# Sixteen tiles in chunks of 2, 3, 4, 4 and 3 instead of 4, 4, 4 and 4, and gathers in tens that wait one group behind

## The reference

```python
target = item_id_feat + gelu(_ln(item_emb_d128 @ mm_w + mm_b, mm_ln_g, mm_ln_b))
seq_emb = item_table[item_seq]                      # rows x 50 x 128
x = concatenate([t, seq_emb, t - seq_emb, t * seq_emb], axis=-1)
scores = relu(x @ aw1 + ab1) @ aw2 + ab2            # 512 -> 64 -> 1
weights = softmax(where(item_seq == 0, -1e9, scores), axis=1)
hist_feat = einsum('bs,bsd->bd', weights, seq_emb)
sparse = stack([like, view, item_id, item_img, hist])   # 5 fields
se = sparse * sigmoid(relu(mean(sparse) @ se_w1 + se_b1) @ se_w2 + se_b2)
bil = pairwise (se[i] @ bil_W[i]) * se[j]           # 10 fields
dnn_in = xc = concatenate([se, bil])                # 15 x 128 = 1920 columns
for i in range(2):
    xc = dnn_in * (xc @ cross_K[i] + cross_bias[i]) + xc
h = gelu(_ln(xc @ w1 + b1, ...)); h = gelu(_ln(h @ w2 + b2, ...))
return sigmoid(h @ w3 + b3)
```

## Time and profile before

| | us |
|---|---|
| median of 3 runs | 2170.15 |
| lowest and highest | 2168.94, 2171.7 |
| span of the profiled execution | 2187.8 |

### The profile page before, as it was taken

One profiled execution on the slowest core, in us unless ns is written; L12 is line 12 of the kernel. 1 busy time (PEld: TensorE's weight loads), 2 busy tenths in 40 slices (PEclk: granted clock), 3 DMA queues, 4 the chain that ended last, 5 costly groups with the idle time before them and its releaser, 6 DMA issues. The chain is left out here.

```text
span 2187.8 us, 32802 instructions
## 1 busy us (share of the span) xinstructions
PE 1951.8 (89%) x9608; PEld 1531.8 (70%) x9608; DVE 1332.7 (61%) x2213; ACT 903.1 (41%) x1963; POOL 901.3 (41%) x854
## 2 busy tenths in 40 slices
PE   1654553999999999999999999999999999999997
PEld 1433432777777787777777787777777888888885
DVE  3444444577677766666777665666777755445553
ACT  1332332344454434664444334654445343322223
POOL 6666666566566540555565610545552000000000
PEclk6755565999999999999999999999999999999998
DMA  4111111344343463333344452334433352333330
GB/s 155 43 45 46 42 45 39 110 113 121 105 122 103 133 207 89 85 97 107 109 122 121 119 189 80 89 95 123 121 107 92 106 172 84 87 99 98 97 89 20
DMA packets 99535, 220.31 MB, mean 101 GB/s; under 512 B 21648, under 2 KB 27040, under 8 KB 99232
## 3 DMA queue, kind: packets, MB, share of 16 engines
q1 hardware_dynamic: 62928, 136.90, 21.0%
q0 software_dynamic: 27136, 55.63, 9.9%
q10 hardware_dynamic: 9296, 25.70, 3.1%
HBM read 205.29 MB, written 12.85 MB: 100 GB/s over the span
## 5 line engine op out<-in xcount | busy, mean ns | idle before, releaser
L394 POOL DMA_INDIRECT e<-in_item_table,idx_all x800 | 853.0, 1066 | 703.6 <-issue 340.1
L1087 DVE TENSOR_TENSOR Wl<-raw,Wh 128x640 fp32r<-128x640 f32 (+1 forms) x420 | 338.1, 805 | 297.5 <-DVEq L1086 269.0
L771 ACT ACTIVATE Wh<-raw 128x640 fp32r<-128x640 f32 (+1 forms) x420 | 301.4, 722 | 506.7 <-ACTq L770 430.0
L519 PE MATMUL xps<-X0h,Wh 128*128 128x512 f32 x900 | 365.0, 406 | 6.7 <-issue 6.7
L519 PE MATMUL xps<-X1h,Wh 128*128 128x512 f32 x900 | 361.7, 402 | 1.6 <-PEq L513 1.6
L520 PE MATMUL xps<-X1l,Wh 128*128 128x512 f32 x900 | 352.6, 392 | 0.0
L521 PE MATMUL xps<-X1h,Wl 128*128 128x512 f32 x900 | 352.5, 392 | 0.0
L521 PE MATMUL xps<-X0h,Wl 128*128 128x512 f32 x900 | 352.4, 392 | 0.0
L520 PE MATMUL xps<-X0l,Wh 128*128 128x512 f32 x900 | 351.9, 391 | 0.0
L734 ACT ACTIVATE e<-e,pw 128x128 f32<-128x128 f32 x800 | 242.7, 388 | 15.5 <-ACTq L128 10.5
L519 PEld LDWEIGHTS xps<-X0h,Wh 128*128 128x128 f32 x900 | 170.0, 189 | 40.8 <-issue 8.7
(11 more groups left out here) (144 smaller groups left out, 2233.7 us busy)
## 6 DMA issues: line engine op xcount, KB each, us to landing
raw<-in_cross_K SPq DMA_DIRECT2D x360, 320.0 KB
raw<-in_w SPq DMA_DIRECT2D x60, 256.0 KB
e<-in_item_table,idx_all POOLq DMA_INDIRECT x800
dnn_scratch<-dn ACTq DMA_DIRECT2D x12, 960.0 KB
x1f<-dnn_scratch ACTq DMA_DIRECT2D x3, 2048.0 KB
x1f<-dnn_scratch ACTq DMA_DIRECT2D x3, 1792.0 KB, 14.8
dn<-in_embT SPq DMA_DIRECT2D x1, 1024.0 KB
img_scratch<-dn ACTq DMA_DIRECT2D x1, 1024.0 KB, 4.8
```

The costliest lines, as they stand in the source:

```text
L394: nc.gpsimd.indirect_dma_start(out=dst, out_offset=None, in_=table, in_offset=bass.IndirectOffsetOnAxis(ap=idx_all[:, t, s:s + 1], axis=0) ...
L519: m0 = mm(out, wh, Xh[:, 0:T, k, :], start=(k == 0), stop=False)
L771: af(Wh[:, split_slot(w), 0:n], raw[:, rs, 0:n], ACT.Copy).then_inc(hi_done, 1)
L1087: v.tensor_tensor(Wl[:, rs, 0:n], raw[:, rs, 0:n], Wh[:, slot, 0:n].bitcast(F32), ALU.subtract).then_inc(lo_done, 1)
```

## The change

The 16 tiles are split as 2, 3, 4, 4 and 3, five chunks instead of four; all buffers stay sized for four tiles, since `TPC` is the largest chunk. The gathers of the first five tiles (chunks 0 and 1) wait, after each group of ten is issued, for the group ahead of it in the tile; before, those of the first four tiles waited after each ten for these same ten. The gathers of the other tiles wait after each five for what has been issued in the group, as before.

```diff
@@ -16,7 +16,7 @@
-TILES = (4, 4, 4, 4)
+TILES = (2, 3, 4, 4, 3)
 CHUNKS = len(TILES)
@@ -412,9 +412,12 @@
                     for s in range(g * GRP, (g + 1) * GRP):
                         gather(e[:, s, :], table_d, t, s, e_landed[g])
-                        if (s + 1) % (GRP if t < TILES[0] else SUB) == 0:
+                        if t >= TILES[0] + TILES[1] and (s + 1) % SUB == 0:
 
                             pool.wait_ge(e_landed[g], (t * GRP + s + 1 - g * GRP) * DMA)
+                    if t < TILES[0] + TILES[1] and g:
+
+                        pool.wait_ge(e_landed[g - 1], (t + 1) * (DMA * GRP))
```

## The result

The changed kernel takes 2220.47 us (median of 4 runs, 2216.51 to 2225.77), the kernel before on the same chip 2170.93 (2168.94 to 2171.76). The ratio is 1.0229, with a 95% interval of 1.0212 to 1.0247: slower by 2.3%. The forecast was 2167, its range 2124 to 2208. The profiled execution of the changed kernel took 2217.7 us, 2.1 more than its span.

What follows compares the result with a forecast made beforehand. TensorE bound the old chunks and GpSimd the opening; VectorE would bind the first new chunk, GpSimd the second. Terms 197 + 328 + 425 + 478 + 452 + 305 = 2185 us of span, less 17.6, gave 2167; range 2124 to 2208.

Steps and rivals of the forecast that it cites:

- Opening: Attention alone before the first chunk, now two tiles with fewer gather stalls: the first chunk starts at 197 us.
- Rival D: Opening: gathers in tens don't speed up, as each gather may grow without the stalls; opening 214, time 2184 us; chance 0.10.
- Product cadence: TensorE's spacing of products in the narrower chunks: 0.121 us at 256 columns, 0.174 us at 384.
- Rival E: Narrow products: weight loads add to each one, 0.22 or 0.27 us apiece; time 2302 us or more; chance 0.02.
- C0': First chunk, two tiles of products carrying attention of three: VectorE's chain binds, 328 us.
- light steps: First chunk, three steps of each tile with neither scaling nor reduce to wait for: 7.6, 7.0 and 6.5 us.
- C1': Second chunk, three tiles of products carrying attention of four, gathers in fives: GpSimd becomes the bound, 425 us.
- Rival B: Second chunk: GpSimd isn't the bound; chunk 408 us, time 2150 us; chance 0.13.
- C2': Third chunk, four tiles: like the second and third chunks before, with FC work for one tile less, 478 us.
- C3': Fourth chunk, four tiles of products carrying attention of three: 452 us.
- C4': Fifth chunk, three tiles without attention: 305 us.
- C: First chunk: TensorE's clock falls, a step with a group takes 21.8 us instead of 12.8; time 2176 to 2212; chance 0.15.

Runs made afterwards that it cites:

- tiles_only: The kernel before with the new chunks of 2, 3, 4, 4 and 3 tiles but the old waits of the gathers; ratio 1.0306 against the kernel before.
- tens_to_9: The changed kernel with the gathers of tiles 5 to 8 also issued in tens that wait for the ten ahead; ratio 1.0182 against the kernel before.
- before_again: The kernel before, unchanged, run again with a profile; ratio 1.0003, profiled execution 2167.6 us.
- warm: The changed kernel with extra 128-column matmuls in the 2-tile chunk where TensorE waits, into columns nobody reads; ratio 1.0210 against the kernel before.
- gathers_only: The changed kernel with four chunks of four tiles, keeping the first five tiles' gathers in tens; ratio 0.9818 against the kernel before.

## Why the prediction was wrong

**Opening: right.** 195.4 for 197, with no stall between tens, in GpSimd's timeline of the changed kernel at the spot where the earlier trace rows had 1.77 us:

```profile
20.20 0.94 POOL L394 DMA_INDIRECT e<-in_item_table,idx_all  x1 [0.30 <-issue]
21.44 0.94 POOL L394 DMA_INDIRECT e<-in_item_table,idx_all  x1 [0.30 <-issue]
```

The 1.9 us taken off for each of five stalls a tile are right for two tiles (19 forecast, 17.4 between tiles_only and the changed kernel). Rival D fell.

**Product cadence: right.** 513.00 - 512.88 = 0.12 us at 256 columns and 2100.27 - 2100.10 = 0.17 at 384, where 0.121 and 0.174 were taken. The fifth chunk's 45 x 30 products are inside the window that took 252 us in all. Rival E, products that pay for each weight load, fell, and with it, for this kernel, the rule of the Trainium skill ("TensorE: Matmul & The Clock Gate", "The mechanism") that a load overlaps only a matmul of another row group: all products here use the whole array, and loads of 0.11 us each would have made these pitches 0.22 and 0.27.

**C0', the step that failed in the sum: 357 for 328.** The prediction's own sign, a chunk off its term by over 15 us, says so. The steps that weigh had the chain about right. Reduces in VectorE's timeline of the changed kernel:

```profile
318.49 2.48 DVE L1034 TENSOR_REDUCE acc<-e 128x128 f32<-128x1280 f32 x1 [0.62 <-DVEq L1032]
...
332.81 2.49 DVE L1034 TENSOR_REDUCE hist<-e 128x128 f32<-128x1280 f32 x1 [1.48 <-DVEq L1032]
...
344.08 2.37 DVE L1034 TENSOR_REDUCE hist<-e 128x128 f32<-128x1280 f32 x1 [2.24 <-DVEq L1032]
```

344.08 - 332.81 = 11.3 us, where 11.4 was forecast for weighing alone, and 14.3 over a step with times-target and the pairs, for 12.8 and the pairs. The light steps were mis-sized. I took 7.6, 7.0 and 6.5 us for them, "splits, times-target, gate", as sums of VectorE's own work "with neither wait". But each of the three has a group placed in it, so its times-target waits for that group's second copy, which stands behind the round trip over ScalarE's program order. From x_sum to x_sum in VectorE's timeline, the gate steps of the last two tiles took 11.1 and 12.1, the steps behind them 8.0 and 9.0, the third light ones 7.9 and 10.2. A tile took 91.5 and 96.9 us for the 87.3 forecast, 14 of the 29 us together; the w1 stage with the gap behind it, 28.6 + 3.7 = 32.3 for 26, has 6 more, whose cause no run separates. The last five steps took 35.8 for 31.5: with the split ahead they take 30.4, so this is the split's place. The last 5 lie in the first step and the third tile's steps. The bound of 345, "if each light step also waits for its partner", was too low as well, since it had no term for a copy queued behind another engine's adds.

**C1': right in kind, short by 10.** The gathers of tiles 6 to 8 took 881 - 599.5 = 281 us, as forecast (281.5 to the last one's end), and tens_to_9 shows that they bind. Tile 6 started at 599.54 - 552.7 = 46.8 us into the chunk for 42, and the tail took 434.6 - 46.8 - 283.5 = 104 us for 99: w1 was 36.9 and 2.1 of gap, for 31, the steps ahead of it 3 less than summed. Rival B, "GpSimd isn't the bound", is out for this kernel, since tens_to_9 made C1' shorter, though by 8 us and not by the 17 between my 425 and 408; without that bound and with the round trip mended C1' is 416, not the 408 I gave it.

**C2' and C3'.** The 478 rested on C1 and C2 of the profiled execution, mean 481.5; in before_again they are 472.6, and the same working gives 470 for the measured 466.4. The same correction turns C3' into 443 for 451.2, so its good fit was luck. The fourth chunk has 451.2 - 441.2 = 10 us of idle TensorE, most of it the same wait ahead of a group's second transposes as in C0' (the changed kernel, 1454 to 1905):

```profile
PE aps L439 <- PEq L437: 8.7, 3, 4.2
```

**C4'.** 305 for 310.7, some 5 of it in the products and the FC work (252 us in the window for 247).

**From span to time: the other step that failed.** "The median of the runs is 17.6 under the profiled span, and I keep that." It was the excess of one execution, 12 of its 22 us in one chunk. Kept as an offset it was taken off a sum most of whose terms had not been inflated by it. With the 2 us that lie outside each span, the forecast would have been 2187, still 33 too low.

**The rivals.** C was right in its sign only. The clock does fall in C0', to 0.90 over the chunk, and in the gate step above the first products come 0.21 us apart instead of 0.12 (from TensorE's timeline of the changed kernel):

```profile
395.25 0.42 PE L523 MATMUL xps<-X1l,Wh 128*128 128x256 f32 x1
395.46 0.41 PE L524 MATMUL xps<-X1h,Wl 128*128 128x256 f32 x1
```

It came after TensorE's idle 8.45 us. But in a chunk that VectorE's chain bounds, slow products mostly fill time that TensorE would have waited: warm gave back 2 us for half of the dip. The Trainium skill ("TensorE: Matmul & The Clock Gate", "Why this matters for your kernels") warns that idle gaps between bursts of matmuls bring the clock down. The rows agree, and it was hardly a price here. The case that came true, slower through VectorE's chain and the hand-over between engines, was no rival of mine with a price; its mechanism was in the forecast for the steps that weigh, without the wait in the light ones.

**Where the opening's gain went.** Against gathers_only, which has the same gathers, the changed kernel's opening is 141.6 us shorter (337.0 - 195.4) and its chunks are 227.8 longer (2020.2 - 1792.4). From rows and the forecast's unit prices: the products' fixed part is 17.6 (1350 x (0.120 + 0.174 + 2 x 0.227 + 0.173) less 1350 x 4 x 0.227), the attention of two tiles beside products is 55 (2 x 27.4). The rest, 155, is above the price of the work. C0' has 93 us over its products, w1 and attention (357.3 - 162 - 20.5 - 82), where the first chunk of four tiles has none; C1' has 59 (434.6 - 235 - 31 - 110) for the second chunk's 16. By the windows TensorE is idle 68 us of C0' (60 and 8 in its w1 stage) and 42 of C1' (36 and 6); the others of these us are work that took longer than its price, some of it at the low clock. These two chunks give 136 of the 155; 19 lie in the later chunks and borders. The gain was real, but nearly all of it, 136 of 142 us, went into two chunks whose products are too narrow to cover the attention that they carry, and the attention and the products' fixed part took 72 more.

## What to carry over

In this kernel, making the binding engine's products narrower stopped paying where another engine's chain of one step became as long: work that chain out, with every wait between engines in it, before the gain at the start. In such a chain read each engine's program order as well as its durations, since an old, ready piece of work queued behind something that waits (here a copy behind an add of another engine) costs a round trip as soon as there is no slack. And compare a profiled execution's time with its own span before taking the difference to the median for an offset: here the excess belonged to that one execution, and not to the next kernel.

## What the hardware showed that I had not expected

- One execution of the kernel before had a span 22 us (1%) longer than its later profile, at the same clock (0.926 and 0.927), with over half of it in one chunk, while the medians of that kernel in two sets of runs were 2170.9 and 2172.8.
- A product costs a near constant 13 to 14 ns above its columns at 2.4 GHz: 0.120 for 0.107 at 256 columns, 0.173 for 0.160 at 384, 0.227 for 0.213 at 512, each with a new weight load.
- A granted clock of 0.90 instead of 0.95 over a chunk cost about 2 us of 357, in a chunk that another engine bounded.
- Gathers in tens for four more tiles took 9.0 us off the span, the reordered copy 6.6 (14 in its chunk, of which the next took back some), and the two together 31 (there the copy was reordered in both chunks). The gains did not simply add up.
